# Weights stored in load order, and the W_o projection evacuated by VectorE alone

## What is computed

```python
# mixer
delta = sigmoid(x @ W_t.T + b_t) * 0.99 + 0.01
Bu = x @ W_b.T + b_b
h = scan(exp(A * delta), Bu)                  # over the sequence
y = (h @ W_c.T + b_c) + x * D
y = y @ W_o.T + b_o
# FFN, bitlinear(x, w): scale = mean |w| of each output row; tern = clip(round(w / scale), -1, 1)
#                       returns x @ (tern * scale).T
h = bitlinear(x, w_fc) + gate * (x @ v.T @ fast_b.T @ u.T)
out = bitlinear(relu(h) ** 2, w_proj)
# layer
x = x + mixer(layernorm(x)); x = x + ffn(layernorm(x))
```

## Time and profile before

| | us |
|---|---|
| runs | 2276.32, 2079.71, 2267.56 |
| median of the runs | 2267.56 |
| profiled execution | 2080.67 |
| its span on the slowest core (core 3) | 2079.1 |
| spans of the 8 cores | 2066.1 to 2079.1 |
| TensorE matmuls busy | 1384.2 (67%) |
| VectorE busy | 889.9 (43%) |
| ScalarE busy | 386.7 (19%) |

### The profile page before, as it was taken

How to read it: one execution, slowest core, us unless ns; L and a number is a source line. 1 busy time by engine, 2 the same in 40 slices (tenths; PEclk the granted TensorE clock), 3 DMA queues, 4 the chain that set the end, 5 groups by cost and what they waited for, 6 DMA issues and landing times.

```text
span 2079.1 us, 14944 instructions; the slowest of 8 cores (2066.1 to 2079.1 us)
## 1 busy us (share of the span) xinstructions
PE 1384.2 (67%) x5768; PEld 614.2 (30%) x5768; DVE 889.9 (43%) x933; ACT 386.7 (19%) x464; POOL 26.9 (1%) x42
## 2 busy tenths in 40 slices
PE   1444354324288849883987489758966895698598
PEld 0111154301033314331433134223422342243243
DVE  1777868645622271237124621552164316412410
ACT  1111121112131013112301220122013202210220
POOL 0000000000000000000000000000000000000000
PEclk9766577656599979996998699879977997899799
DMA  6233446341021513241324123412431151235033
GB/s 126 101 121 121 120 143 182 111 152 41 0 104 73 189 40 122 72 171 41 122 83 160 60 103 107 153 60 85 154 129 54 68 183 60 72 110 182 28 114 142
DMA packets 73237, 221.44 MB, mean 107 GB/s; under 512 B 4512, under 2 KB 37280, under 8 KB 54720
## 3 DMA queue, kind: packets, MB, share of 16 engines
q1 hardware_dynamic: 60208, 167.79, 24.1%
q0 software_dynamic: 12960, 52.69, 7.1%
HBM read 189.28 MB, written 33.55 MB: 107 GB/s over the span
## 4 chain that ended last, share of the span: by engine, by line
PE 58%; DVE 27%; ACT 5%; issue 4%; DMA 4%; DVEq 0%; POOL 0%; ACTq 0%; POOLq 0%; SPq 0%
PE pb L975 21%; PE pb L920 21%; PE pb L770 6%; PE pb L357 3%; PE pb L442 2%; DVE tls L889 2%; DVE tls L623 2%; DVE xnb L633 2%; DVE xnb L899 2%; DMA wsl<-wprojT 2%; DVE cb L383 2%; DVE sqbuf L553 2%; DVE cb L384 2%; DMA woT_b<-woT 1%; PE pb L561 1%
## 5 line engine op out<-in xcount | busy, mean ns | idle before, releaser
L920 PE MATMUL pb<-xnb,wcmb_st 128*128 128x512 bf16 x2048 | 474.6, 397 | 139.7 <-DVE but L659 86.7
L975 PE MATMUL pb<-r2b,wproj_st 128*128 128x512 bf16 x2048 | 443.5, 379 | 0.1
L920 PEld LDWEIGHTS pb<-xnb,wcmb_st 128*128 128x128 bf16 x2048 | 206.3, 101 | 408.3 <-issue 187.3
L975 PEld LDWEIGHTS pb<-r2b,wproj_st 128*128 128x128 bf16 x2048 | 200.3, 98 | 242.0 <-issue 1.2
L950 DVE TENSOR_TENSOR r2b<-r2b 128x4096 bf16<-128x4096 bf16 x32 | 73.3, 2292 | 388.4 <-ACT r2b L941 388.4
L941 ACT ACTIVATE r2b<-pb 128x512 bf16<-128x512 f32 x256 | 152.1, 597 | 289.8 <-PE pb L920 289.7
L993 DVE TENSOR_TENSOR xn<-xn,pb 128x512 f32<-128x512 f32 x64 | 44.0, 687 | 365.3 <-PE pb L975 365.3
L770 PE MATMUL pb<-yb,woT_b 128*128 128x512 bf16 x512 | 129.3, 417 | 13.6 <-DVE yb L749 12.5
L561 PE MATMUL pb<-xb,ones_b 128*128 128x512 bf16 x64 | 28.6, 626 | 130.0 <-DVE xb L554 130.0
L304 PE MATMUL pb<-GTb,v_b 16*128 16x512 bf16 x64 | 22.1, 450 | 115.3 <-DVE wr L311 115.2
L780 ACT ACT_TABLE_LOAD x8 | 10.3, 1283 | 460.0 <-PE pb L770 460.0
(11 more groups left out here) (110 smaller groups left out, 1202.2 us busy)
## 6 DMA issues: line engine op xcount, KB each, us to landing
wcmb_st<-wcmb_sc SPq DMA_DIRECT2D x64, 1024.0 KB, 4.9
wproj_st<-wproj_sc SPq DMA_DIRECT2D x64, 1024.0 KB, 4.9
x_s<-xT POOLq DMA_DIRECT2D x8, 2048.0 KB, 8.5
yT<-xn POOLq DMA_DIRECT2D x8, 2048.0 KB, 8.8
wsl<-wfcT SPq DMA_DIRECT2D x4, 2048.0 KB, 11.0
wslB<-wfcT SPq DMA_DIRECT2D x4, 2048.0 KB, 11.0
wcmb_sc<-wr POOLq DMA_DIRECT2D x8, 1024.0 KB, 4.2
wsl<-wprojT SPq DMA_DIRECT2D x4, 2048.0 KB, 12.2
```

What stands on the lines that cost most here:

```text
L920: i2 = te.matmul(pb[b][:], wcmb_st[:, hs % 2, dc, (hc % 4) * 128:(hc % 4 + 1) * 128], xnb[:, p, dc], start=(dc == 0), stop=(dc == DCH - 1))
L975: i2 = te.matmul(pb[b][:], wproj_st[:, oc % 2, kc, :], r2b[:, kc], start=(kc == 0), stop=(kc == hch - 1))
```

## The change

Two independent parts.

The host lays w_fc and w_proj out slice by slice in the order in which a slice lies in SBUF: wfcT becomes [8 slices, 128 partitions, 8, 512] and wprojT [8 slices, 128 partitions, 32, 128]. Each load then reads 16 KB in one piece for each partition. The sizes, the buffers, the queue and the waits stay.

In the W_o stage ScalarE has no work left. VectorE waits for each group of matmuls and computes (PSUM + bias) + x_s in one scalar_tensor_tensor straight into `xn32`. TensorE waits for VectorE's count where it waited for ScalarE's; since the first half's square counts as well, the counts are 1, 2, 3, 4, then 6, 7, 8, 9 (`STTN`). `tls` isn't used here any more, and what follows no longer waits on this stage for it.

```diff
-    wfcT = nc.dram_tensor("wfcT", [D, h], F32, kind="ExternalInput").ap()
-    wprojT = nc.dram_tensor("wprojT", [h, D], F32, kind="ExternalInput").ap()
+    wfcT = nc.dram_tensor("wfcT", [nhs, 128, DCH, TT], F32, kind="ExternalInput").ap()
+    wprojT = nc.dram_tensor("wprojT", [DCH, 128, hch, 128], F32, kind="ExternalInput").ap()
...
-            inc(sy.dma_start(
-                out=wv[:],
-                in_=wfcT[:, hs * TT:(hs + 1) * TT].rearrange("(c p) h -> p c h", p=128),
-            ), wldq(hs), 16)
+            inc(sy.dma_start(out=wv[:], in_=wfcT[hs]), wldq(hs), 16)
...
-            inc(sy.dma_start(
-                out=wv2[:],
-                in_=wprojT[:, os_ * 128:(os_ + 1) * 128].rearrange("(c p) o -> p c o", p=128),
-            ), wldq(j), 16)
+            inc(sy.dma_start(out=wv2[:], in_=wprojT[os_]), wldq(j), 16)
...
-        S1 = ctr["s_S"]
-
-        def _wo(te, j=j, S1=S1):
+        STTN = [1, 2, 3, 4, 6, 7, 8, 9]
+
+        def _wo(te, j=j, V1=V1):
             wait(te, "tensor", "s_V", yb_done[j])
             for oc in range(DCH):
                 b = 4 + oc % 2
                 if oc >= 2:
-                    wait(te, "tensor", "s_S", S1 + oc - 1)
+                    wait(te, "tensor", "s_V", V1 + STTN[oc - 2])
...
-        def _wo_evac(sc, j=j):
-            wait(sc, "scalar", "s_V", run["tls"])
-            for oc in range(DCH):
-                b = 4 + oc % 2
-                wait(sc, "scalar", "s_T", wod[oc])
-                inc(sc.activation(out=tls[:, oc], in_=pb[b][:], func=AF.Identity,
-                                  bias=bo_s[:, oc:oc + 1]), "s_S")
-        blk.scalar(_wo_evac)
...
             for g2 in range(2):
-                wait(ve, "vector", "s_S", S1 + 4 * g2 + 4)
-                last = None
                 for q in range(4):
                     oc = 4 * g2 + q
-                    last = ve.tensor_tensor(out=xn32[:, p, oc], in0=tls[:, oc],
-                                            in1=x_s[:, p, oc], op=ALU.add)
-                inc(last, "s_V")
+                    b = 4 + oc % 2
+                    wait(ve, "vector", "s_T", wod[oc])
+                    inc(ve.scalar_tensor_tensor(out=xn32[:, p, oc], in0=pb[b][:],
+                                                scalar=bo_s[:, oc:oc + 1],
+                                                in1=x_s[:, p, oc],
+                                                op0=ALU.add, op1=ALU.add), "s_V")
...
-        wo_stt_done[j] = run["wo_stt"] = run["tls"] = ws = ctr["s_V"]
+        wo_stt_done[j] = run["wo_stt"] = ws = ctr["s_V"]
```

More of the change, by code:

```diff
@@ L773, in emit_back1, with _wo_stt @@
         blk.tensor(_wo)
-        def _wo_evac(sc, j=j):
-            wait(sc, "scalar", "s_V", run["tls"])
-            for oc in range(DCH):
-                b = 4 + oc % 2
-                wait(sc, "scalar", "s_T", wod[oc])
-                inc(sc.activation(out=tls[:, oc], in_=pb[b][:], func=AF.Identity,
-                                  bias=bo_s[:, oc:oc + 1]), "s_S")
-        blk.scalar(_wo_evac)
         wo_mm[j] = dict(wod)
         sqh = {}
-        def _wo_stt(ve, j=j, S1=S1):
+        def _wo_stt(ve, j=j):
             if j >= 2:
@@ L1061, in make_in_maps @@
                  fast_b, w_fc, w_proj, u, v, gate, spc=SEQ_PER_CORE):
+    nhs_, hch_ = w_fc.shape[0] // TT, w_fc.shape[0] // 128
     shared = dict(
-        wfcT=np.ascontiguousarray(w_fc.T),
-        wprojT=np.ascontiguousarray(w_proj.T),
+        wfcT=np.ascontiguousarray(
+            w_fc.T.reshape(DCH, 128, nhs_, TT).transpose(2, 1, 0, 3)),
+        wprojT=np.ascontiguousarray(
+            w_proj.T.reshape(hch_, 128, DCH, 128).transpose(2, 1, 0, 3)),
         woT=np.ascontiguousarray(W_o.T),
```

## The result

| | before | after |
|---|---|---|
| median of the runs | 2081.66 us (10 runs) | 2055.25 us (9 runs) |
| profiled execution | 2080.67 us, span 2079.1 | 2053.11 us, span 2051.6 |
| spans of the eight cores | 2066.1 to 2079.1 | 2038.1 to 2051.6 |

The ratio of the times is 0.9865, with a 95% interval of 0.9853 to 0.9878. Forecast were 2053 us and 0.987. Some executions of each of these kernels take 2 to 9% longer, with a lower granted clock on one die or both (the highest are 2276.32 us before and 2214.76 after); the medians count them, here and in the experiments, and the ratios and intervals leave them out.

A forecast was written before the change was run, and what follows sets the result against it. TensorE's chain, 58% of the time, was taken as the bound. From 2080.67 us, 11.7 for the weight loads and 16.0 for the W_o stage were subtracted, giving 2053 us, ratio 0.987, range 2037 to 2068.

The forecast's parts named there:

- The w_proj loads (-11.7): Weight preparation: three w_proj loads on the chain shrink from 13.44, 8.95 and 13.26 us to 8 each, saving 11.7 us.
- L: Length of one w_proj load on the chain after the change; taken as 8 us, bounds 7.5 and 11.0.
- The w_fc loop (0): Weight preparation: TensorE and VectorE hide the w_fc loads, so their new layout gains 0.
- bounds of -3.2 and +2: Kernel start: woT_b lands up to 3.2 us earlier, or some 2 us later if longer runs are served ahead; taken 0.
- x_s (0): Before the first tile: x_s's landing time after issue, 17.78 us on core 3, taken as unchanged; bounds -4.4 and +1.
- The W_o stage (-15.2): W_o stage of all 8 tiles: the second square starts 1.9 us earlier in each, 15.2 us in all.
- the 0.8 of the first and last tile: W_o stage: TensorE's 0.48 us idling before its third group, for ScalarE, goes in two tiles; 0.8 us for both.
- the loads stay long: Rival for the w_proj loads: shared memory held them, not the runs; loads 11 to 12 us, time 2062 to 2065; chance 0.15.
- VectorE delays TensorE more: Rival in the W_o stage: TensorE waits 1.5 us behind the square instead of 0.65; time 2060; chance 0.08.
- The clock: Rival in the W_o stage: the new hand-over keeps TensorE's clock at 0.50, 81 us more, time 2134; chance 0.03.
- sign of wrong, 0.50 later than 4 us: W_o stage: a granted clock of 0.50 later than the stage's first 4 us would show the prediction wrong.
- More than forecast: Rival across preparation and W_o stage: shorter loads, earlier x_s and woT_b, 2.54 us a tile; time 2039; chance 0.12.

The follow-up runs named there:

- experiment 1: Changed kernel with both new weight layouts but the W_o stage going through ScalarE as before; 2078.07 us, ratio 0.9991 against the kernel before.
- experiment 4: Changed kernel with each w_proj slice in one piece of 2 MB but still read in runs of 512 B; 2060.18 us, ratio 0.9912.
- experiment 12: Changed kernel with each w_proj slice in one piece of 2 MB, read in eight runs of 2 KB per partition; 2056.44 us, ratio 0.9882.
- experiment 11: Changed kernel with the dropped wait put back, VectorE's next use of `tls` waiting for the W_o stage's end; 2055.97 us, ratio 0.9878.
- experiment 2: Changed kernel with both weights back in the old layouts, keeping the new W_o stage; 2057.77 us, ratio 0.9889.
- experiment 7: Changed kernel with woT_b on a semaphore of its own, for which only the W_o matmuls wait; 2042.27 us, ratio 0.9806.
- experiment 9: Changed kernel with w_fc's old layout, first half's square behind group 5's evacuation, woT_b's own semaphore and first x tile loading alone; 2024.44 us, ratio 0.9719.

## Why the prediction was right, and where

The time was right to 2 us by the medians (to 0.2 between the profiled executions), and that closeness is luck, because two errors of 6 us cancelled: the preparation gave 5.2 us of 11.7, and the tiles 22.3 of 16.0.

**The w_proj loads (-11.7): mis-sized.** The place and the cause were right. The loads' length sets this loop, runs of 512 B are slower (experiments 1, 4 and 12), and L came to 8.9 us in the mean where I took 8. The rule that I weighed (the Trainium skill, DMA: Bandwidth & Descriptors, section Specifications: 512 B are enough for line rate) would have left the loads as they were. No run here bears it out with eight cores loading at once: 11.1 us with 512 B against 8.9. A window over one load of after shows the same; its columns are those of the earlier trace rows, for VectorE, and 399 GB/s stand there against 290:

```profile
319.00:322.00 3.00, 2.45 (x4) 1.00 0.98 399
```

What failed is the other side of the subtraction. "13.44 + 8.95 + 13.26 - 24" takes the three loads of the slowest core. That core was the slowest because its loads came out long in that execution; with shorter loads the draw falls differently, and some core has the longest again. With the mean of all cores the term is 3 x (10.9 - 8.9) = 6 us. The odd slices' loads, which the prediction kept off the chain, gave some of it back: TensorE's idle time before them rose by 5.2 us.

**The w_fc loop (0): the step was right, its neighbour not.** The loop did hide its loads. But I put the place where they do harm, beside woT_b and the constants, at 0 with bounds of -3.2 and +2. It was +1.9, the side on which long runs are served ahead. For woT_b's own landing that is 1.2 us on core 3 (31.78 against 30.55), and the rest is in TensorE's column sums in the w_fc loop (the first 8.83 us instead of 8.49). That the small constant is delayed by 13 us on core 3 I had not seen at all, and it is hidden only as long as woT_b lands later still.

**x_s (0): right.** On the slowest core it took 18.27 us, against 17.78.

**The W_o stage (-15.2): right in its mechanism, with one term too small.** The operation took 749 ns (745), TensorE waited 0.61 us (0.65), the second square came at 17.5 us (17.9), and ScalarE and its table load were gone. With the 0.8 of the first and last tile 16.0 were forecast for this stretch; it was 18.2. The mis-sized term is those 0.8. TensorE's wait for ScalarE's table and first evacuation was taken from the row of 0.48 us and counted for two tiles; it held the third group in all eight, 2.3 us in all (the section on the result has the rows), and in the middle six it is mostly too short for a row. The clock's sooner rise gives some 1.8 more. The wait before group 6, 0.77 by the distance of the groups and not 0.65, takes 1.0 back: 16.0 - 0.8 + 2.3 + 1.8 - 1.0 = 18.3, against the 18.2.

**What the sum didn't have.** First, the `tls` wait, 1.2 us (experiment 11). The diff shows it, and I passed over it. Second, the FFN's first half starts at a better clock. Windows of TensorE in the 10 us ahead of its first Relu and the 6 us from there on (span, us busy, matmuls, clock, DMA share, GB/s), in one tile before:

```profile
1175.02:1185.02 10.00, 5.73 (x16) 0.67 0.00 0
1185.02:1191.02 6.00, 5.26 (x15) 0.59 0.00 0
```

and in after, in the same tile and in the one with the slow start:

```profile
1157.61:1167.61 10.00, 5.14 (x16) 0.83 0.01 2
1167.61:1173.61 6.00, 5.26 (x18) 0.72 0.00 0
...
1554.24:1564.24 10.00, 6.49 (x16) 0.67 0.00 0
1564.24:1570.24 6.00, 5.26 (x13) 0.50 0.00 0
```

Ahead of the Relu it is 16 matmuls each time, in 5.73, 5.14 and 6.49 us. Behind it TensorE does 18 matmuls in 6 us at 0.72, 15 at 0.59 and 13 at 0.50. With the statistic stage this is 3.1 us over the kernel, and 5.2 in experiment 2, which has no slow tile. Why the clock rises sooner, and why single tiles start slowly, stays open. Third, 2.2 us were given back in the FFN's second half, where TensorE now waits in some tiles for a transfer of w_proj's weights (`wproj_st`): its idle time before L961 is 1.4 us on the page after, 1.2 of it for that transfer, where it was 0.1 before.

**The rivals.** That the loads stay long fell with experiments 1 and 4. That VectorE delays TensorE more fell with the row of 0.61 us. The clock didn't fall again within the stage: on core 3 it rises to 1.00 at 2.7 to 4.8 us into it (3.3 to 4.5 before) and stays there. The prediction's sign of wrong, 0.50 later than 4 us, was met in both kernels by rises of up to 4.5 and 4.8 us and so told nothing. "More than forecast" happened in the tiles alone.

## What to carry to other kernels

When an evacuation or an addition is collected into groups, look at the last group: the work behind the last matmul stands on the chain, and doing it piece by piece gave 1.8 of 2.3 us here with the old engines still in place. Longer runs made a transfer faster here at the expense of what was in flight beside it, so before a layout is changed, look at which small constant or first weight is waited for in the same microseconds; here a semaphore of its own for the late weight (12 us) and the first tile alone (7 us) were worth more than both layouts. And a term that subtracts a transfer's time should take the mean over all cores, not the slowest core's. And ScalarE's table load held TensorE here almost without an idle row: what showed it is a start that stays the same from tile to tile while the clock ahead of it doesn't.

## What the runs showed that I had not expected

- A transfer of 0.5 KB took 7.7 us in the mean of the cores (8.2 on core 3) beside w_fc loads in 2 KB runs, and 18.3 (21.1 on core 3, 26.27 on core 0 in experiment 7) beside loads in 16 KB runs; single cores still had it after some 5 us.
- Of cores 0 and 1, 2 and 3, 4 and 5, 6 and 7, the one that issues x_s later waits the longer for it, before and after: 17.7 to 18.3 us, the other 13.4 to 16.5. With the first tile alone (experiment 9) it is 10.4 to 11.5 us on all cores. Why pairs, no run here shows.
- If the instruction behind VectorE's cast waits for VectorE's own count, though the cast stands just ahead of it, it starts 0.2 us later (2.39 against 2.21).
- The same matmuls at the start of the FFN's first half take 57.0 to 58.7 us by how soon the clock rises, from tile to tile of one execution.
